# One root for sixteen tiles, sums off GpSimd, and earlier block requests in a fused quantised-FFN kernel

## What is computed

```python
xn = (x - mean(x, -1)) / sqrt(var(x, -1) + 1e-5)
# attention over the 4 "batch" rows for each of 1024 last-axis positions
q = transpose(xn, (2, 0, 1))
s = xn + transpose(softmax(q @ q.T / sqrt(1024)) @ q, (1, 2, 0))
# FFN: Wg, Wu are (2752, 1024), Wd is (1024, 2752); W = NF4[codes] * scale
ffn = (silu(xn @ Wg.T) * (xn @ Wu.T)) @ Wd.T
out = x + s * silu(ffn)
```

## Time and profile before

| | us |
|---|---|
| timed runs, median of 3 | 2653.19 |
| lowest, highest | 2650.83, 2657.51 |
| the profiled execution | 2647.06 |
| its span, first to last instruction | 2645.3 |

### The profile page before, as it was taken

One profiled execution on the slowest core, in us unless ns is written; L12 is line 12 of the kernel. 1 busy time (PEld: TensorE's weight loads), 2 busy tenths in 40 slices (PEclk: granted clock), 3 DMA queues, 4 the chain that ended last, 5 costly groups with the idle time before them and its releaser, 6 DMA issues.

```text
span 2645.3 us, 30451 instructions
## 1 busy us (share of the span) xinstructions
PE 2440.1 (92%) x11214; PEld 1113.7 (42%) x11214; DVE 1671.4 (63%) x2929; ACT 1011.9 (38%) x1303; POOL 166.1 (6%) x110
## 2 busy tenths in 40 slices
PE   2459999998899898999999999999999999999999
PEld 1224444443344343444444444444444444444444
DVE  6767887977688765787888788656451331341341
ACT  5467766657576643445445442111001001001000
POOL 3540000000000000000000000000011011011011
PEclk9689999998899899999999999999999999999999
DMA  6254565756566538666565654325877767766864
GB/s 221 100 172 157 187 195 179 221 179 203 182 204 196 195 128 331 214 225 203 185 215 190 202 192 171 129 85 201 335 285 281 322 263 275 324 267 270 326 267 159
DMA packets 176017, 571.15 MB, mean 216 GB/s; under 512 B 23968, under 2 KB 49232, under 8 KB 158076
## 3 DMA queue, kind: packets, MB, share of 16 engines
q1 hardware_dynamic: 140876, 280.82, 31.2%
q10 hardware_dynamic: 34992, 288.37, 29.0%
HBM read 380.38 MB, written 188.75 MB: 215 GB/s over the span
## 4 chain that ended last, share of the span: by engine, by line
PE 68%; DVE 12%; DMA 7%; issue 6%; ACT 3%; POOL 2%; SPq 2%; DVEq 0%; POOLq 0%; ACTq 0%
PE ps L1560 38%; PE ps L1689 29%; DMA arena<-xnsc 3%; DVE arena L1226 3%; DMA isc<-arena 2%; DVE arena L1160 1%; ACT arena L727 1%; POOL arena L680 1%; DVE arena L1135 1%; SPq L505 1%; DMA arena<-in_gu 1%; DVE arena L1219 1%; DVE arena L1394 1%; DVE st L1075 1%; DMA xsc<-arena 1%
## 5 line engine op out<-in xcount | busy, mean ns | idle before, releaser
L1560 PE MATMUL ps<-arena 128*128 128x512 f16 x7200 | 1595.5, 384 | 107.6 <-ACT arena L902 52.1
L1560 PEld LDWEIGHTS ps<-arena 128*128 128x128 f16 x7200 | 710.2, 99 | 980.7 <-ACT arena L902 58.4
L1689 PE MATMUL ps<-arena 128*128 128x512 f16 x3696 | 797.9, 379 | 0.0
L727 ACT ACTIVATE arena<-arena,bias_t 128x1024 f32<-128x1024 f32 (+1 forms) x520 | 574.3, 1141 | 53.2 <-DMA arena<-in_gu 33.7
L1689 PEld LDWEIGHTS ps<-arena 128*128 128x128 f16 x3696 | 361.6, 98 | 436.3 <-issue 0.4
L1226 DVE TENSOR_TENSOR arena<-arena 128x512 f16<-128x512 f32 x364 | 248.9, 686 | 72.7 <-ACT arena L861 71.2
L692 POOL TENSOR_TENSOR arena<-arena 128x512 f32<-128x512 f32 x64 | 81.8, 1286 | 2376.4 <-DMA arena<-in_xt 2072.7
L1043 ACT ACTIVATE arena<-arena,e_d 128x512 f32<-128x512 f32 x48 | 34.6, 721 | 424.3 <-DVE arena L1489 219.4
L902 ACT ACTIVATE arena<-ps,gate_back 128x512 f32<-128x512 f32 x84 | 57.3, 682 | 348.2 <-PE ps L1560 348.2
L1219 DVE CAST arena<-arena 128x512 f16<-128x512 f32 x308 | 126.5, 421 | 40.8 <-DMA isc<-arena 38.3
L912 ACT ACTIVATE arena<-arena,gate_back 128x512 f32<-128x512 f32 x84 | 60.4, 720 | 208.6 <-DVE arena L1391 179.7
(11 more groups left out here) (109 smaller groups left out, 1203.3 us busy)
## 6 DMA issues: line engine op xcount, KB each, us to landing
isc<-arena SPq DMA_DIRECT2D x308, 256.0 KB, 2.4
arena<-wdsc ACTq DMA_DIRECT2D x28, 2816.0 KB, 10.2
arena<-isc ACTq DMA_DIRECT2D x28, 2816.0 KB, 18.2
arena<-xnsc SPq DMA_DIRECT2D x48, 1024.0 KB, 10.4
wsc<-arena ACTq DMA_DIRECT2D x21, 1792.0 KB, 6.2
arena<-in_gu ACTq DMA_DIRECT2D x43, 512.0 KB, 4.2
wdsc<-arena SPq DMA_DIRECT2D x77, 256.0 KB, 2.3
arena<-in_x SPq DMA_DIRECT2D x32, 512.0 KB, 6.9
```

The costliest lines, as they stand in the source:

```text
L727: a_.activation(buf, src, ACT.Prelu, bias=bias_t[:, i:i + 1], scale=scale, alpha=alpha).then_inc(ramps, 1)
L1560: ins = t_.matmul(ps[:, bank, :], wreg[:, b, w, wa, k, :], xreg[:, j, o, k, xa, :], start=start and (k, wa, xa) == (0, 0, 0), stop=stop an ...
L1689: ins = t_.matmul(ps[:, bank, :], ring_w[b][:, k, wa, g, :], ring_i[b][:, k, xa, :], start=first and (k, wa, xa) == (0, 0, 0), stop=r not ...
```

## The change

1. **Scales.** The host lays all block scales out in one array with a row of 4,128 bytes for each partition; one DMA replaces five.
2. **Layer norm.** Statistics of all sixteen tiles 0 to 15 are taken first, then one `roots` works out 16 inverse deviations. VectorE normalises nine of the tiles and ScalarE seven (5, 6, 7, 12 to 15) with scale and bias. GpSimd has no part in the opening but the first constants and the reduction of the scales.
3. **Early sets.** The sums are VectorE's (`early_made`), in three groups instead of five; set 4 is cast by VectorE too. All sets use PSUM banks 0 to 3 and tiles 8 to 15 banks 4 to 7, so the tiles' transposes stand between those of the sets, ahead of pass 0. Sets 4 and 5 stand in pass 0 and beside weight tile 1, sets 6 and 7 in pass 1, and pass 2 takes its operands along as they are made.
4. **Tiles 16 to 31.** Their statistics are taken in passes 4, 6 and 7, one tile in a slot, from a load of their own; one `roots` stands in slot 1 of pass 8. `NORM_AT` moves from passes 6 to 20 to passes 8 to 22, and is only the scaling now, one tile in each of slots 4 and 5. Each of these tiles is loaded twice.
5. **x jobs.** They move to passes 26, 27, 30, 31, 34, 35, 38, 39. Those of the even passes are made by VectorE alone, all 18 pieces in slots 0 to 2 (`SOON_CUT`); the others still have ScalarE's casts. Blocks are requested one pass earlier: for the even one at the top of the pass before, for the odd one behind the stores of the even one.
6. **ScalarE's order.** Half of a pass's ramps now stand before the weight's high parts; `reloads` is dealt out over four places of a pass. The requests for the first down scales move from pass 40 to 43, and the down items of pass 44 to slot 5.

```diff
-NORM_AT = {6 + 2 * i: (16 + 2 * i, 17 + 2 * i) for i in range(8)}
-XJOB_AT = {s: (2 + i // 4, i % 4) for i, s in enumerate([s for s in SPARE if s >= 22][:8])}
+STAT_AT = {4: range(16, 22), 6: range(22, 27), 7: range(27, 32)}
+ROOTS_AT = 8
+NORM_AT = {8 + 2 * i: (16 + 2 * i, 17 + 2 * i) for i in range(8)}
+XJOB_AT = {s: (2 + i // 4, i % 4) for i, s in enumerate([s for s in SPARE if s >= 24][-8:])}
+X_ACT = [XJOB_AT[s] for s in XJOB_AT if PASS[s][1]]
...
-EARLY_OPS = [[0], [1, 2], [4, 5], [3], [6]]
+EARLY_OPS = [[0], [1, 2], [3, 4, 5, 6]]
+NG = len(EARLY_OPS)
+EARLY_HERE = [4]
+SOON_CUT = [0, 8, 13, 18, 18, 18, 18]
...
-            sp.dma_start(s_g[:, 0:FT, :], gate_scales[0:FT * P, :].rearrange("(i p) b -> p i b", p=P)).then_inc(scales_in, 16)
...
+            sp.dma_start(s_all, scales).then_inc(scales_in, 16)
...
+            for tt in range(8, 16):
+                load_nat(tt)
             sp.wait_ge(sc_out, 9 * 16)
...
-                if s in XJOB_AT:
-                    load_blocks(("x",) + XJOB_AT[s])
+                if s + 1 in XJOB_AT and s not in XJOB_AT:
+                    load_blocks(("x",) + XJOB_AT[s + 1])
...
                 for c in jobs_at(s):
                     for o in X_ORDER:
                         store_stage(c, o)
+                if s + 1 in XJOB_AT and s in XJOB_AT:
+                    load_blocks(("x",) + XJOB_AT[s + 1])
...
+                if s == 3:
+                    load_stat(16)
+                    load_stat(17)
+                for tt in STAT_AT.get(s, ()):
+                    if tt + 2 < 32:
+                        load_stat(tt + 2)
...
+            def load_stat(tt):
+                h, n, q = tokens(tt)
+                if tt < 18:
+                    sp.wait_ge(e_lo, NG * 7)
+                else:
+                    sp.wait_ge(stat, 32 + 2 * (tt - 18) + 2)
+                sp.dma_start(nat[nat_slot(tt)], x[n, h * CH + q * P:h * CH + (q + 1) * P, :]).then_inc(nat_in[nat_slot(tt)], 16)
...
-            lnorm_share([5, 6, 7])
-            for e in range(4):
-                early_sums(e)
-            lnorm_share([13, 14, 15])
-            for e in range(4, NEARLY):
-                early_sums(e)
...
+            def normal(tt):
+                i = tt % 16
+                if tt == NORM_ACT[0]:
+                    act.wait_ge(shift_made, 1)
+                a_.activation(nat[nat_slot(tt)], nat[nat_slot(tt)], ACT.Identity, bias=shift[:, i:i + 1],
+                              scale=y[:, 1, i:i + 1]).then_inc(xn_act, 1)
...
+                if (s, part) == (42, 0):
+                    act.wait_ge(prod, prod_at(41, "r"))
+                    act.wait_ge(prod, prod_at(40, "p3"))
+                    load_xb(0, 0)
+                elif (s, part) == (42, 1):
+                    load_xb(0, 4)
...
-            for s in range(1, TOTAL + 1):
+            for s in range(2, TOTAL + 1):
...
-                if s in XJOB_AT:
+                on_act = s in XJOB_AT and XJOB_AT[s] in X_ACT
+                if on_act:
                     for o in (0, 1, 2):
                         x_high(("x",) + XJOB_AT[s], o)
...
+            def early_made(e):
+                early_sums(e)
+                if e in EARLY_HERE:
+                    for g in range(NG):
+                        if g == 2:
+                            dve.wait_ge(ep_made, 4 * e + 4)
+                        v_.tensor_copy(early_dest(e, g, 0), early_source(e, g)).then_inc(eh_here, 1)
+                for g in range(NG):
+                    early_low(e, g)
...
-                if s == 0 and slot == 3:
-                    lnorm(range(8, 16), 5)
-                if s in NORM_AT and slot == 3:
-                    lnorm(NORM_AT[s], 2)
+                for tt in list(STAT_AT.get(s, ()))[slot:slot + 1]:
+                    stats(tt)
+                if s == ROOTS_AT and slot == 1:
+                    dve.wait_ge(xn_act, len(NORM_ACT))
+                    dve.wait_ge(stat, 64)
+                    roots()
+                if s in NORM_AT and slot >= 4:
+                    normal(NORM_AT[s][slot - 4])
...
+            for tt in range(16):
+                stats(tt)
+            dve.wait_ge(stat, 32)
+            roots()
...
+            early_made(3)
+            first_half(0)
+            early_made(4)
+            second_half(0)
+            for i in range(13):
+                w_item(1, i)
+            early_made(5)
+            first_half(1)
+            early_made(6)
+            early_made(7)
```

More of the change, by code:

```diff
@@ L196, in ramp_count, with build @@
     return w_base(w, 2 * NR, NR) + ramp_order(w).index((tile, i)) + 1
-def build(nc, x, xt, gu_codes, d_codes, gate_scales, up_scales, down_scales, out):
+def build(nc, x, xt, gu_codes, d_codes, scales, out):
     NB, C, H = x.shape
-    I = gate_scales.shape[0]
+    I = 2752
     KT = H // P
@@ L916, in _ @@
             act.wait_ge(bias_set, NR)
-            for n in range(4):
+            for n in range(8):
                 ramp(0, n)
@@ L1206, in c_item @@
                 src, d = operand_of(c, o), dest(c, o)
+                on_act = c[0] == "x" and c[1:] in X_ACT
                 if what == "t":
@@ L1321, in background @@
                 for c in jobs:
-                    for i in range(JOB_CUT[slot], JOB_CUT[slot + 1]):
+                    at = SOON_CUT if c[0] == "x" and c[1:] not in X_ACT else JOB_CUT
+                    for i in range(at[slot], at[slot + 1]):
                         c_item(c, i)
@@ L1326, in background @@
                     w_item(u, i)
-                if s in EARLY_AT and slot == 5:
-                    for e in EARLY_AT[s]:
-                        for g in range(5):
-                            early_item(e, g)
-                if s in DOWN_AT and slot == (5 if jobs else 1):
-                    d_items(*DOWN_AT[s])
-                if s == 0 and slot == 3:
-                    lnorm(range(8, 16), 5)
-                if s in NORM_AT and slot == 3:
-                    lnorm(NORM_AT[s], 2)
+                if s in DOWN_AT and slot == (5 if jobs or s == NSTEP else 1):
+                    d_items(*DOWN_AT[s])
+                for tt in list(STAT_AT.get(s, ()))[slot:slot + 1]:
[6 more added lines that the diff above has]
+                    normal(NORM_AT[s][slot - 4])
                 if s in GRAM_AT and slot == 3:
@@ L1575, in _ @@
             ins.then_inc(sct_done, 1)
-            for e in range(4):
+            early_transposes(0)
+            for e in range(1, 4):
                 early_transposes(e)
+                for tt in (6 + 2 * e, 7 + 2 * e) if e < 3 else (12, 13, 14, 15):
+                    half_tile(tt, 0)
+                    half_tile(tt, 1)
             def free_bank(s, name):
-                if s == 1 and name in ("p1", "p7", "p5"):
-                    pe.wait_ge(xe_done, {"p1": 13, "p7": 14, "p5": 15}[name])
+                if s == 0 and name in FIRST:
+                    pe.wait_ge(ee_done, 8)
+                elif s == 1 and name in ("p7", "p5"):
+                    pe.wait_ge(xe_done, {"p7": 13, "p5": 14}[name])
+                elif s == 1 and name == "p1":
+                    pe.wait_ge(q_made, 1)
                 elif name == "p1":
@@ L1706, in gu_tiles @@
         return c[:full].reshape(21, 128, 8, 128).transpose(0, 3, 2, 1)
+    gs, us, ds = (_np.asarray(inputs[f"L0_ffn_{k}_scales"]) for k in ("gate", "up", "down"))
+    sc = _np.concatenate([
+        _np.concatenate([gs, us[full:]]).reshape(22, 128, 16).transpose(1, 0, 2).reshape(128, -1),
+        us[:full].reshape(21, 128, 16).transpose(1, 0, 2).reshape(128, -1),
+        ds.reshape(8, 128, 43).transpose(1, 0, 2).reshape(128, -1)], axis=1)
     gu = _np.empty((43, 128, 8, 128), gate.dtype)
```

421 lines of the change are left out of this document (235 added, 186 removed).

## The result

The changed kernel takes 2581.35 us, median of 4 runs (2580.22 to 2583.09), against 2653.97 for the kernel before beside it: a ratio of 0.9727, 95% interval 0.971 to 0.9743. The forecast was 2553, the range 2526 to 2596. The direction and two of the four terms, the opening and passes 4 to 21, came out near their values; the x jobs, the largest, and the turn did not. The profiled execution took 2580.2 us with a span of 2578.3.

What follows compares the result with a forecast made beforehand. TensorE, busy 92% of the span, was taken as the bound, with its waits to be gained. 24.5 + 10 + 56 + 9 = 99.5 us off the profiled 2647.1 gave 2547.6; timed runs lie 6 above: 2553, range 2526 to 2596.

Steps and rivals of the forecast that it cites:

- the opening: Term for the start up to pass 4: pass 4 starts at 192.5 instead of 217.0 us, 24.5 us gained, bounds 10 to 34.
- passes 4 to 21: Term for these passes: most c21 waits go as VectorE's layer norm work shrinks; 10 us gained, from 2 lost to 16.
- the x jobs: Term for the eight x jobs: silA waits vanish in four, 0 to 3 us in the others; 56 us gained, bounds 35 and 64.
- the turn: Term for 899 to 1080 us, where the halves turn: reloads one at a time hold stores less; 9 us gained, 0 to 15.
- the likeliest case: The forecast itself over the whole kernel: 2553 us, spanning 2535 to 2572, chance 0.62.
- the two slower rivals: Opening gives nothing, 2578 us, and odd x jobs still stall, 2581 us; chance 0.14 each.
- the sum of the good ends: All parts of the kernel at their good end: 34 + 16 + 64 + 13 = 127 us, 2526; chance 0.07.
- a sign of "wrong": In passes 4 to 7, waits for statistics above 3 us would show the prediction wrong.
- The odd jobs stalled: Rival for the odd x jobs: four of eight stalls stay, 9 us each less 2 counted, 28 us, 2581; chance 0.14.
- VectorE as the bound of every pass: Rival for passes 4 to 39: VectorE bounds each pass, 5.5 us a pair erases the gain, 2671 at 6.5; chance 0.03.
- The opening without gain: Rival for the start up to pass 4: its 24.5 us don't come, 2578 us; chance 0.14.

Runs made afterwards that it cites:

- Experiment 11: The changed kernel with the four sums of each early set on GpSimd again, the rest of the opening as changed: 2603.2 us, ratio 0.9808.
- experiment 10: The changed kernel without the tile requests of passes 3 to 7, statistics of tiles 18 to 31 taken from tiles 16 and 17: 2570.8 us, ratio 0.9694.
- Experiment 4: The changed kernel with the even x block's request behind the fourth store of the pass ahead, instead of ahead of all seven: 2564.3 us, ratio 0.9676.
- Experiments 6 and 7: On Experiment 4: x pairs' scale spreads moved behind the odd pass's second store, 2565.0 us; then also the odd block requested behind VectorE's last block read, 2561.2 us.
- experiment 3: The changed kernel with each x block requested in its own pass and all x casts on ScalarE: 2621.2 us, ratio 0.989.
- experiment 1: The changed kernel with the casts of the four even x jobs back on ScalarE, early requests kept: 2599.1 us, ratio 0.9807.
- Experiment 8: The changed kernel with the reloads of passes 41 to 45 in one row at the top of each pass: 2576.7 us, ratio 0.9713.
- experiment 9: Experiment 8 with the scale spreads of the first down weight back in pass 40 instead of 43: 2583.4 us, ratio 0.9743.

## Why the prediction was right, and where it was wrong

The time is 28 us over the forecast and lies outside the 2535 to 2572 of the likeliest case; it is inside the whole range because the two slower rivals had stretched that to 2596, and neither of them came about. So the range held in part by luck, and the four terms have to be judged one by one. Two slips of the working change nothing: the sum of the good ends counts 13 us for the turn, whose bound was 15, and TensorE's dips in the earlier trace rows are slices 10, 11, 14 and 16, not 15.

**The opening, 24.5 forecast, 25.8 measured: right, and for the reasons given.** The statistics started at 10.45 (forecast 11), the last ended at 40.6 (38), pass 0 started at 97.7 (94.5), and q of pass 2 came at 165.7 (166). Of the 3 us by which pass 0 came late, 1.2 were left at the copy of p1 (107.2, forecast 106) and 0.7 at the end of the ramps (123.7, forecast 123). ScalarE's seven normalising activations took 1.245 us each in the mean, beside 1.142 for the ramp by which I had priced them: 0.10 more. That the second pointer operand costs some 0.09 us is what the Trainium skill says (ScalarE: Activation LUTs, "What ACT_TABLE_LOAD costs"); these rows agree. Experiment 11 shows that most of the gain needs the sums' move.

**Passes 4 to 21, 10 forecast, 8.3 measured: right in size.** TensorE waited for c21 in passes 6 and 7, by up to 6.7 us where I had said that one comes some 2 late, and nowhere from pass 8 to 21. The landing is the cause, as put (experiment 10). Two waits for statistics (3.13 and 3.65 us) are above the 3 us that I had set as a sign of "wrong", so by my own sign this part failed; the term still held, since the long landing came in three slots (the third 2.87) and not in all.

**The x jobs, 56 forecast with bounds 35 and 64, 32.5 measured: this is the step that failed.** It is this sentence: "For the even job the new request stands a whole pass ahead, so the landing is hidden, and ScalarE has no casts", with "8 us lost where 64 were". The landing is hidden from the job, and that was right: of the eight waits for silA two short ones are left, 2.8 us in the stage. But I let the request itself cost nothing. It is put ahead of seven stores, and its 1 MB runs together with 1 MB of scales and with those stores; VectorE, which has four buffers for them, waits 3.4 to 4.8 us for a store once in each of passes 25, 29, 33 and 37, and with the casts in its list hands that on as late c21s (19.9 us). I had seen a wait for a store behind other transfers at the turn, but didn't look for one here. Experiment 4 gives 10.4 us of the stage back by moving this request alone. The second part is the odd block. I had it 4 to 9 us into the odd pass; it took 9.5 us from request to first cast, 12.4 in kernel 4, beside the spreads. Experiments 6 and 7 take 9.1 us more out of the stage. The stage is then 340.7 us, so 52.1 are gained of the 56 forecast.

**What I had credited to the request alone belonged in good part to the casts.** The table behind experiment 3 says it: with the casts of the even jobs on VectorE, the request a pass ahead, ahead of the stores, gives 2 us, which is within scatter; only behind the fourth store does it give 19. In the forecast the casts on VectorE were a price of 2.3 us a pass, and I gave them no gain of their own but that ScalarE is rid of them. Undoing them costs 18 us with the early requests and 38 without. With them the odd block is requested sooner and also lands sooner; only the first is explained, by the one buffer.

The Trainium skill (Perfetto Trace Analysis, "Optimizing Scalar/DVE Operations") says that off a saturated VectorE some work may go to ScalarE or even GpSimd, and adds that between GpSimd and VectorE this might not help, since they share a read port. VectorE is busy for 83% of passes 22 to 35 of the changed kernel, 229.5 of 277.5 us, so it isn't saturated in the mean, and no run tests the first part; here taking the casts off VectorE cost 18 us (experiment 1). Experiment 11 agrees with the second part: giving the sums to GpSimd cost 22 us, with 1446 ns for a low part that takes 684 otherwise.

**The turn, 9 forecast, 2.5 measured: the size and the reason were wrong.** Kernels with the same turn scatter by 4.4 us there, so the 2.5 is rough, but no such kernel reaches the 9. I laid the 9.3 us of the earlier trace rows on four reloads issued in a row. Experiment 8 puts them in a row again and loses nothing; experiment 9 brings the wait back with the four spreads of scales, which the change had moved too. At the turn the changed kernel's TensorE waits 4.04 us for c21, where it had waited 10.69, but 4.06 us of issue have come up (2.5 in kernel 8), where there had been 2.0.

**The rivals.** The odd jobs stalled: 2581, the time that came, but by another road; it wanted four stalls for silA of 9 us, and there were seven small ones for c21. A right number for this rival would have been a coincidence. VectorE as the bound of every pass is excluded: in the changed kernel as in experiment 10 TensorE ran without a wait from pass 8 up to pass 24, and in kernel 4 it waits only 2.2 us for c21 in the x stage, in which every pass has a job from 24 on. The opening without gain is excluded by the marks.

## What to carry to other kernels

A request that is moved ahead isn't free once its landing is hidden: ask which stores and loads are in flight where it now starts, and how many buffers the engine behind them has. Here it cost 10 us in the stage, and moving it behind the fourth store brought them back. Where one buffer serves two jobs, ask of an edit also when it frees the buffer, and test two edits that attack one stall in all four combinations, since their gains don't add: 38 and 22 gave 40.

## What the runs showed of the hardware that I had not expected

- A store of 256 KB has a median of 2.4 us to landing over the whole kernel, but 7.1 us in the 14 us behind the block's request in pass 25, and 5.0 in the same 14 us of kernel 4. With the block on ScalarE's queue, and asked for 8 us sooner, the median behind its request was 8.7 us in this pass and 5.5 to 7.0 in the three others.
- Beside GpSimd's sums of 128x512 float32, VectorE's subtraction of the same shape took 1446 ns in the mean instead of 684, and its multiplication over 1024 elements 2288 instead of 1218.
- One unchanged stretch, 1486 to 1490 us long from pass 50 to the end, scattered by 4 us between profiles. A gain of 3 us in a stage can be read in the profile and still not be found in the time.
